# A graph network's gathers written out with fixed index columns, and six more groups of rows gathered ahead

## What is computed

```python
# layers one and two (8 heads, then 1 head): a graph attention layer
feat = (h @ fc_w.T).reshape(n, heads, out_feats)
e = leaky_relu(el[src] + er[dst], 0.2)
a = softmax of e over the edges with equal dst
rst = segment_sum(feat[src] * a[..., None], dst)
h1 = relu(h0 + norm * (inputs @ wb0.T + bb0))            # behind layer one
out = h2 + norm * (concat([inputs, h1]) @ wb1.T + bb1)   # behind layer two, the residual
# layer three: attention with 4 heads and a relation for each edge type
scores = einsum("ehd,ehd->eh", Q[dst], K[src] + 0.2 * rel[:, None, :]) / D ** 0.5
agg = segment_sum(softmax(scores)[:, :, None] * V[src], dst)
out = layernorm(where(deg > 0, agg, V) @ Wo + bo + node_features) * gamma + beta
```

## Time and profile before

| | |
|---|---|
| median of 3 runs | 2544.82 us (2539.74 to 2546.16) |
| the profiled execution's span | 2542.8 us |
| PE busy | 1609.3 us (63%), 7823 instructions |
| DVE busy | 1510.8 us (59%), 2311 |
| ACT busy | 417.4 us (16%), 809 |
| POOL busy | 1567.7 us (62%), 2569 |
| DMA | 408.99 MB, 161 GB/s over the span |
| GpSimd's gather queue, share of the 16 engines | 29.0% |
| SP's queue, share of the 16 engines | 24.1% |

### The profile page before, as it was taken

How to read it: one execution, slowest core, us unless ns; L and a number is a source line. 1 busy time by engine, 2 the same in 40 slices (tenths; PEclk the granted TensorE clock), 3 DMA queues, 4 the chain that set the end, 5 groups by cost and what they waited for, 6 DMA issues and landing times. The chain is left out here.

```text
span 2542.8 us, 32600 instructions
## 1 busy us (share of the span) xinstructions
PE 1609.3 (63%) x7823; PEld 1196.9 (47%) x7824; DVE 1510.8 (59%) x2311; ACT 417.4 (16%) x809; POOL 1567.7 (62%) x2569
## 2 busy tenths in 40 slices
PE   6426556556557446655556568977777767389965
PEld 5314334344346444544444433655545445267743
DVE  3446756756765886433333365565656565679968
ACT  1100000000004000000000025333433333110114
POOL 0588888888812888888888701888888888100013
PEclk9657777777777557877777789877776777589989
DMA  3634334334314553333333324899999999667702
GB/s 98 144 98 110 107 103 110 108 103 111 96 28 144 157 152 112 110 104 103 105 103 101 95 68 135 280 299 291 302 295 298 295 298 291 244 216 272 246 27 75
DMA packets 238175, 408.99 MB, mean 161 GB/s; under 512 B 33651, under 2 KB 174892, under 8 KB 231468
## 3 DMA queue, kind: packets, MB, share of 16 engines
q0 software_dynamic: 73216, 219.89, 29.0%
q1 hardware_dynamic: 164907, 188.55, 24.1%
HBM read 333.82 MB, written 74.48 MB: 161 GB/s over the span
## 5 line engine op out<-in xcount | busy, mean ns | idle before, releaser
L854 POOL DMA_INDIRECT row_space<-tab_feat,index_slot x680 | 677.9, 997 | 174.5 <-issue 102.3
L1128 PE MATMUL ps<-arena 128*128 128x257 f32 (+1 forms) x1664 | 466.8, 445 | 208.5 <-DVE arena L1962 208.5
L1128 PEld LDWEIGHTS ps<-arena 128*128 128x128 f32 x1664 | 367.2, 226 | 306.9 <-issue 236.8
L854 POOL DMA_INDIRECT row_space<-tab_kv,index_slot x384 | 372.9, 971 | 101.2 <-issue 59.8
L1956 DVE TENSOR_TENSOR arena<-row_space,ps 128x2048 f32<-128x2048 f32 x101 | 230.4, 2281 | 289.4 <-DMA row_space<-tab_feat,index_slot 289.4
L1224 PE MATMUL ps<-arena 128*128 128x265 f32 x832 | 263.9, 485 | 115.3 <-DVE ps L2186 56.7
L1068 PE MATMUL ps<-acc,arena 128*128 x832 | 307.0, 533 | 0.0
L1224 PEld LDWEIGHTS ps<-arena 128*128 128x128 f32 x832 | 198.6, 245 | 168.7 <-issue 123.2
L1844 DVE TENSOR_TENSOR arena<-row_space,ps 128x1024 f32<-128x1024 f32 x104 | 126.7, 1218 | 208.6 <-DMA row_space<-tab_kv,index_slot 177.8
L1453 ACT COPY acc<-ps 128x265 f32<-128x265 f32 (+2 forms) x75 | 28.3, 377 | 1326.2 <-PE ps L1128 672.0
L1068 PEld LDWEIGHTS ps<-acc,arena 128*128 128x128 f32 x832 | 210.9, 266 | 43.7
(11 more groups left out here) (336 smaller groups left out, 2308.5 us busy)
## 6 DMA issues: line engine op xcount, KB each, us to landing
item_v<-row_space SPq DMA_DIRECT2D x52, 1024.0 KB, 6.5
row_space<-item_v SPq DMA_DIRECT2D x52, 1024.0 KB, 4.9
arena<-rows_block_dst SPq DMA_DIRECT2D x104, 128.0 KB
row_space<-tab_feat,index_slot POOLq DMA_INDIRECT x808
scores<-rows_block_dst SPq DMA_DIRECT2D x52, 128.0 KB
arena<-rows_src_low SPq DMA_DIRECT2D x52, 128.0 KB
arena<-rows_type SPq DMA_DIRECT2D x52, 128.0 KB
row_space<-tab_kv,index_slot POOLq DMA_INDIRECT x416
```

The costliest lines, as they stand in the source:

```text
L854: nc.gpsimd.indirect_dma_start(rows_of_slot(s)[:, g, :], None, table, bass.IndirectOffsetOnAxis(ap=index_slot[:, s, g:g + 1], axis=0),).th ...
L1128: last = nc.tensor.matmul(ps[:, SUM_BANKS:2 * SUM_BANKS][:, bass.ds(bs[g], 1), 0:width].rearrange("p a d -> p (a d)"), onehot[:, s % 2, g, ...
```

## The change

`gathers` is written out. There is no copy and no loop: each of the 416 gathers of a layer names its column in `src_i` as a constant, and the only wait is the one for the slot ahead of each group (in layer three also the one for the stored values). `index_slot`, `spare_index`, `slot_claimed`, the wait for the copy and the wait for landed gathers are gone.

In layer two, six groups (`AHEAD`) are gathered before the ring's first pass into places of their own: three in `acc` (its start and its end), three in `base` (behind block 0). They are the stage's first six groups, the ring holds the next 43, the spare places the last three. DVE's `sums` takes the six in straight code and runs its loop over five turns of eight, then six groups in straight code. Since ACT writes sums to `acc` in the same stage, it now waits for two made groups ahead of each copy (three from block 17 on); since DVE writes residuals to `base`, it waits for its own rows to be made ahead of the first three.

```diff
-RING_GROUPS = [GROUPS, GROUPS - SPARE, GROUPS, GROUPS]
+AHEAD = 6
+RING_GROUPS = [GROUPS, GROUPS - AHEAD - SPARE, GROUPS, GROUPS]
...
-        index_slot = sb("index_slot", [P, 2 * SLOTS, GROUP], I32)
-        spare_index = sb("spare_index", [P, SPARE, GROUP], I32)
...
+        ahead_places = [acc_flat[:, 0:ROWS], acc_flat[:, ROWS:2 * ROWS], acc_flat[:, ACC_END - ROWS:ACC_END],
+                        base_flat[:, D:D + ROWS], base_flat[:, D + ROWS:D + 2 * ROWS],
+                        base_flat[:, D + 2 * ROWS:D + 3 * ROWS]]
+        HIGH_BLOCK = (ACC_END - ROWS) // AW
...
-                def gather(u, s, ends):
-
-                    ahead = u + (s + 1) // ring, (s + 1) % ring
+                def gather(u, s):
+
                     pool.wait_ge(slot_used[s], u + (uses(n, s) + 1))
-                    if n == 2:
+                    if n == 2 and u:
                         pool.wait_ge(values_stored[s], u * 16)
-                    index(u, s, 0)
-                    pool.wait_ge(pool_step, u * (ring * GROUP) + ((s + 1) * GROUP + step.n))
-                    if not ends:
-                        landed(*ahead)
-                    pool.sem_inc(slot_claimed, 1)
                     for g in range(GROUP):
+                        item = (first + u * ring + s) * GROUP + g
                         nc.gpsimd.indirect_dma_start(
                             rows_of_slot(s)[:, g, :], None, table,
-                            bass.IndirectOffsetOnAxis(ap=index_slot[:, s, g:g + 1], axis=0),
+                            bass.IndirectOffsetOnAxis(ap=src_i[:, item:item + 1], axis=0),
                         ).then_inc(gathered[s], 16)
-                        if g + 1 < GROUP and not ends:
-                            index(*ahead, g + 1)
...
+                for k in range(first):
+                    gather_ahead(k)
                 for s in range(ring):
-                    loose(s)
-                for k in range(GROUPS - mine):
+                    gather(0, s)
+                for k in range(GROUPS - mine - first):
                     gather_spare(k)
...
-                with nc.gpsimd.Fori(0, turns - 1) as u:
-                    for s in range(ring):
-                        gather(u + 1, s, False)
-                for s in range(rest):
-                    gather(turns, s, s + 1 == rest)
+                for i in range(ring, mine):
+                    gather(i // ring, i % ring)
...
                     act.wait_ge(bank_free, n * BLOCKS + b + 1)
+                    if n == 1:
+                        act.wait_ge(weighted_made, GROUPS + (3 if b >= HIGH_BLOCK else 2))
...
+                        if u is None and i < ahead:
+                            dve.wait_ge(weighted_made, GROUPS + i + 1)
```

More of the change, by code:

```diff
@@ L345, in graph_layers @@
         spare_in = [sem(f"spare_rows_gathered{k}") for k in range(SPARE)]
+        ahead_in = [sem(f"ahead_rows_gathered{k}") for k in range(AHEAD)]
         values_stored = [sem(f"values_stored{s}") for s in range(SLOTS)]
         values_in = [sem(f"values_loaded{s}") for s in range(2 * SLOTS)]
-        slot_claimed = sem("rows_slot_claimed")
         parts_made = sem("attention_term_parts_made")
@@ L822, in gathers @@
             def gathers(n, table, name):
-                ring, mine = RINGS[n], RING_GROUPS[n]
-                turns, rest = (mine - 1) // ring, (mine - 1) % ring + 1
+                ring, mine, first = RINGS[n], RING_GROUPS[n], AHEAD if n == 1 else 0
                 pool.wait_ge(phase["sp"], STAGES.index(name) + 1)
@@ L875, in gather_spare @@
                 def gather_spare(k):
                     for g in range(GROUP):
[L878 to L881 removed]
+                        item = (first + mine + k) * GROUP + g
                         nc.gpsimd.indirect_dma_start(
                             spare_rows[k][:, g, :], None, table,
[L884 removed]
+                            bass.IndirectOffsetOnAxis(ap=src_i[:, item:item + 1], axis=0),
@@ L885, in gather_spare @@
                         ).then_inc(spare_in[k], 16)
+                for k in range(first):
+                    gather_ahead(k)
                 for s in range(ring):
-                    loose(s)
-                for k in range(GROUPS - mine):
+                    gather(0, s)
+                for k in range(GROUPS - mine - first):
                     gather_spare(k)
-                step.add(-ring * GROUP)
-                landed(1, 0)
-                for g in range(1, GROUP):
-                    index(1, 0, g)
@@ L1930, in sums @@
                 begin(dve, name, ["pe", "act"])
-                ring, turns, rest = RINGS[nth_pass], GROUPS // RINGS[nth_pass], GROUPS % RINGS[nth_pass]
+                ring, ahead = RINGS[nth_pass], AHEAD if nth_pass == 1 else 0
+                turns, rest = (GROUPS - ahead) // ring, (GROUPS - ahead) % ring
                 did(vec.memset(weighted[:, :, :, DEG:AW], 1.0))
```

73 lines of the change are left out of this document (35 added, 38 removed).

## The result

The changed kernel takes 2299.2 us (median of 4 runs, 2296.7 to 2300.4) where the kernel before takes 2543.2 (2539.7 to 2546.2, 4 runs): a ratio of 0.905, 95% interval 0.903 to 0.906. It gained 244 us; the prediction said 152, with a range that ended 56 us above the result. The direction was right, the size was wrong. In this document a time is the median of all executions of a kernel, and a ratio is taken from those within 1.5% of its fastest one.

The account below looks back on a forecast made before the run. GpSimd's issue rate in three serial stretches of 416 gathers was taken as the bound; 69 (layer two) + 59 (layer one) + 24 (attention scores) = 152 us off 2544.8 gave 2393 us, range 2355 to 2445.

Parts of the forecast that it names:

- the step of 1.25 us: All three gather stretches: one gather without a copy takes 1.25 us (0.95 busy, 0.30 idle), against 1.33 in a loop.
- a border costs nothing: Between groups of eight gathers: no extra time after the change, since the copy's latency and three waits all go.
- GpSimd never stands in layer two with the groups ahead: Layer two: with 17 places instead of 11, GpSimd would not stand from about 969 to 980 us.
- the rest stays: Stages without gathers (node stages, soft, sum3, final): unchanged, nothing gained.
- DVE did catch up: Layer two: DVE needs under 4 us of a group's 11.3, so it catches up at GpSimd's 10.2 us too.
- I read it as service: Score3: DMA share 0.94 at 295 GB/s taken as real service, so 10.97 us a group and minus 24 us.
- the DMA engines have room: Rival in score3: it goes at the issue rate, 59 instead of 24 us gained, 2358 us; chance 0.15.
- The rule of the Trainium skill that the prediction set against the share: Score3: HBM yields some 358 GB/s to one core, fabric ceiling 435, so 295 GB/s would leave room.
- Fetches in straight code, 0.02 us a step: All gathers: rare stops, taken for program fetches, add 0.02 us a step, making it 1.27 us.
- The hold-up by DVE, kept whole: Gathers and copies slowed by DVE's instructions: kept unchanged, 49 us in layer two and 2.5 us a chunk in layer one.
- The groups ahead: Layer two: six groups gathered ahead bring about 11 of the stage's 69 us, the unrolling 58.
- The rival on the slower side: GpSimd's straight program: fetches make it a loss from 7.6 us each, about 2593 us at 10 us each; chance 0.02.

Follow-up runs that it names:

- that part alone: Kernel before with only the attention's 416 gathers written out without copies: 2471.5 us, ratio 0.972 on chip 3; 1.024 and 1.028 on chip 7.
- two stores a group: Changed kernel with score3 cut to its transfers (no TensorE products or DVE work there) and every group's values stored a second time: 2347.6 us.
- the pauses for landed groups: Changed kernel with each group's gathers waiting until the group before has landed, chip 13: 2761.0 us, ratio 1.055 to the kernel before.

## Why the prediction was wrong

**What was right.** That the three rows of 416 gathers bound the kernel and that each gather's step lies on the path; the step of 1.25 us; that a border costs nothing; that GpSimd never stands in layer two with the groups ahead (7.8 us of waiting for a slot in the whole kernel, at the fifth group of score3, as foreseen); that the rest stays (3 us behind the gathers). DVE did catch up.

**The step that failed most: "I read it as service".** The DMA engines were taken as full at 295 GB/s and a share of 0.94, hence 10.97 us a group and 24 us gained. Score3 ran at 1.25 us a gather: 68.7 us in the two traces, 69.2 us with that part alone. The argument was that a byte cost the same share at a load of 0.83 and 0.94. But it costs less at a higher one: q0's 83.61 MB took 59.1% of 400 us, 354 GB/s for full engines where 321 stood, and with two stores a group q1's price fell from 324 (53.09 MB in 40.9%) to 354 GB/s (63.69 MB in 60.0% of 300 us). I read that so: a packet's time holds waiting that other packets can use. The traces show the falling price, not its reason. So the rival "the DMA engines have room", which had 0.15, was the case, and 35 of the 92 us that were missed are the difference between it and the forecast. GpSimd with score3's transfers alone (518.7 us at the issue rate, 341 GB/s) and with a second store (398 GB/s) shows the room; the attention part alone (69.2 us) shows what it is worth. A view of the kernel before spoke for it, and the prediction doesn't rest on it: the throughput in 40 slices of 1 us each, from 1700 us on, with slices at 409 and 410 GB/s.

```profile
GB/s 262 234 251 376 367 314 215 250 349 410 315 266 293 272 351 384 322 137 201 343 409 389 283 209 126 322 386 382 321 223 264 399 203 262 156 190 148 369 389 360
```

A transfer mix that runs at 410 in some microseconds isn't at its limit with 295 in the mean; mean and best slice should have been the two bounds of that term. The best slice is an upper bound only: with two stores a group slices of 1 us reach 434 GB/s (1600 to 1640 us) where the mean is 399.

```profile
GB/s 410 371 420 417 373 393 418 411 393 388 399 411 379 390 408 424 386 397 391 410 410 394 406 390 413 397 389 418 415 385 398 390 420 397 381 382 434 392 378 399
```

The rule of the Trainium skill that the prediction set against the share ("DMA: Bandwidth & Descriptors", section on where 436 GB/s comes from) was the better guide in its direction, though the 358 GB/s that it gives for HBM was passed here. The Trainium skill's page "Perfetto Trace Analysis", in the roofline part of "Engine Utilization", says that one core alone can go beyond its 358 GB/s, up to some 435; the 398 GB/s of the kernel with two stores agree.

**Fetches in straight code, 0.02 us a step.** The changed code has none: not one gather in 1165 had over 0.3 us ahead of it. The term was 8 us in each layer, 16 us in the sum, and it would have been some 8 us more in score3 had the issue rate been forecast there. The stops of the earlier trace rows, 1.26 us ahead of a gather that took 2.03 us among them, were real, but they are not the loops': they stay at the same gathers when the loops are written out, and they are gone from the changed kernel, which neither copies nor waits. Whether they are fetches is open. The Trainium skill ("Runtime: NRT & Kernel Launch", section on instruction fetch) has it that straight code is streamed nearly for nothing, and the changed kernel agrees (0.3 us at most); the prediction named that and set the stops against it. That a taken branch can stall isn't seen here, since the loops brought 6.1 us at most.

**The hold-up by DVE, kept whole.** "It belongs to DVE's instructions, which do not change" was half true. The part that fell on the copies went with the copies. GpSimd's busy time in the first 141 us of layer two is

```profile
723.00:864.00 141.00, 115.28 (x84) 0.50 0.61 171
```

so 84 gathers were held up 115.28 - 84 x 0.95 = 35.5 us, where 64 gathers and their copies had been held up 44.6. In all, layer two's gathers took 558.7 us against the 577 forecast: 8.3 of fetch, 10 of hold-up. Layer one's chunk took 41.3 us (L2090 stands at 206.60 and, nine chunks on, at 578.13) and not 43.1: 0.6 of fetch and 1.2 of hold-up, some 18 us in ten chunks and 5 in the first 64 gathers.

**The groups ahead** were given 11 us and brought 22.8. The stop was to be from 969 to 980 us; it was 25.4 us, because the 88 gathers ahead of it were done 148 us after the first and not 159 (the two terms above), and DVE's first slot came free 173 us behind it, not 170. In the sum this isn't an error of its own, since the total of the stage was forecast without a stop, and there was none.

Together: 23 us in layer one, 20 in layer two, 45 in score3, 3 behind the gathers and 5 ahead of the first, 96 us between the two profiled executions and 92 between the medians. Of the 5, 3.1 are the first copy and what followed it, a term the sum put at nothing. All errors but the 2 us of scatter at the start and the 3 at the end go one way, since each term had been rounded to the careful side; the range counted only one of them, the room of the DMA engines, and so ended at 2355.

**What no case had.** That the same kernel loses 250 us on one chip and 345 on another. The rival on the slower side was another (fetches); nothing in the traces of the first chip points to late signals of TensorE, since there none is late.

## What to carry to other kernels

Before a resource is taken as full from its busy share, look at its best short slices, and put both into the range: here 295 in the mean and 410 in the best microsecond. When an instruction goes, what held it up goes with it, and so does the wait for its result, which was dearer (some 116 us) than the instruction beside each gather (103 us). And time a change that packs an engine's issue on more than one chip: this one is 9.5% faster in the first comparison and on chip 3, and 11 to 13% slower on chips 13 and 7. A stop without a shown reason isn't the loop's until the run without the loop says so.

## What the runs showed of the hardware

- An indirect gather of 128 rows costs GpSimd 0.95 us and 0.30 us to the next, 1.25 us, in runs of over 300 as in runs of seven, for rows of 256, 264 and 512 numbers alike; a small copy between two makes it 1.33 us.
- The 16 DMA engines carried 398 GB/s over 515 us in the mix of 2 KB rows gathered and 1 KB pieces stored, at a share of 1.06; at 341 GB/s they already showed 1.00.
- With copies or waits between gathers, GpSimd stopped for 0.5 to 1.9 us, mostly at every 64th gather of 1 KB rows and every 96th of 2 KB rows, in a loop and in straight code alike (17 and 14 stops); in the unbroken rows of the changed kernel in the first comparison and on chip 3 it never did. The cause is open.
- On chips 7 and 13 TensorE's signals arrived up to 86.6 us late in the densest rows of gathers, and up to 35.8 us late with the old copies and waits; of VectorE's at most two an execution were over 1 us late (by 1.3 us), of ScalarE's none. The same executions have far fewer records of landed transfers than packets that announce one (12,757 of 31,087 for the changed kernel on chip 7; 30,975 in the first comparison), more with the pauses for landed groups (18,556). What in these chips does it is open. Of TensorE's 517 signals, 20 to 63 have no record there. One reading is that the recording of the executions itself is what gets clogged there and holds the engine with the most records back (15,647 instructions of TensorE's, 2311 of VectorE's); every execution here has a recorded span and clock, so none tells it apart, and it wasn't tried. The Trainium skill ("NOTIFIC — the notification-queue block", section on overflow) states that this block can stall an engine when a queue or an internal buffer fills; no run here shows its counters.
